# Top-k norm statistics taken in the window phase, reciprocals two sequences at once, and a new step order in the packed attention of two layers

## The chip, the cores and the metric

The kernel runs on one core of one Trainium2 chip. The metric is the device time of one execution in microseconds; each kernel has a median over its runs. The profile and the trace come from one separate profiled execution of the same program.

## The reference

64 sequences of 128 tokens and 128 channels pass through three transformer layers and a final mixture of experts. `T`=128 tokens, `C`=128 channels, `S`=77 context tokens, `H`=16 heads of `D`=8. What bears on the change:

```python
# layer 0
h = _ln(x) * (1 + sc_msa) + sh_msa
x = x + _self_attn(h) * g_msa             # windows of 64 tokens, shifted by 32
h = _ln(x) * (1 + sc_mca) + sh_mca
x = x + _topk_cross_attn(h, ctx) * g_mca  # softmax over the 16 largest of 77 scores
x = x + _swiglu(...) * g_mlp
# layers 1 and 2
x = x + gate_a * (attention(modulate(_ln(x))) @ W_proj + b)      # 128 keys
x = x + attention(_ln(x), keys and values from context) @ W + b  # 77 keys
x = x + gate_m * mlp(modulate(_ln(x)))
```

`_ln` subtracts the mean over the channels and multiplies by one over the root of the variance plus 1e-6.

## The kernel before, in words

The phases follow each other: setup, window attention of layer 0, top-k attention of layer 0, MLP, then twice (layers 1 and 2) a packed attention and an MLP, then the mixture of experts. x stays in SBUF (`r.x`). All phases work on groups of `G`=4 sequences, so there are `NG`=16 groups. Each engine has an instruction list of its own, in one order written out by hand: a body per group with steps `u`, in which pieces of several groups are interleaved; semaphores couple the engines.

**Window and top-k phases** (`attention_phase`). A window body has 8 steps, a top-k body 16. In the top-k phase the vector engine does four MAX8 and four MATCH_REPLACE8 twice in each step (`find_top`), and per body the norm statistics of the group two ahead (`ln_stats`, L743; `ln_variance`, L774 and L777), a reciprocal per sequence (`reciprocals`, L879) and one add to x (L927). GpSimd turns the variance into one over the root (`rstd_of`, L488, then L491 and L493) and multiplies the rows by the reciprocals (`divide_rows`, L515). ScalarE applies the norm (`ln_apply`, L581).

**Packed attention** (`packed_attention_layer`). `NT`=32 groups pass through it: 16 of self attention (128 keys), then the same 16 of cross attention (77 keys). A body has `NS`=8 steps, two to a sequence. In a step TensorE does 8 matmuls of the scores (L1616, into `s_ps`) interleaved with 8 of the transposed scores of the step 7 before (L1631), in 32-row tiles; VectorE reduces the two halves of the scores to maxima (L1491, two TENSOR_REDUCE per step); ScalarE takes the exponentials of the transposed scores (L1374, two per step); TensorE multiplies them with the values (L1656, 16 matmuls). `s_ps` has one buffer for each half, so before it writes a step's scores TensorE waits until both maxima of the step before are taken:

```python
def scores_waits(g, u):
    ...
    after(pe, s_max, 2 * (NS * g + u))
```

Around that, each body has these pieces at fixed steps: transpose of the normed rows (`XT`, L1584), keys (`KP`, L1592), queries (`QP`, L1597) and values (`VP`, L1604) of the group two ahead, transpose of the attention output (`ONT`, L1752), its projection (`PROJ`, L1756), and the transpose back with the add to x (L1681 at step 0, L1527 at step 1). Keys and queries are split in a high and a low part: ScalarE writes the high part (L1349, L1355), VectorE the low part (`low_keys` L1466, `low_queries` L1471); TensorE starts the queries only when the low part of the keys is there, since all use one PSUM bank `l_ps`. At even steps two transposes of output rows (L1667) come too, at odd steps a transpose of the maxima (L1642). SyncE's queue copies keys and queries to their 32-row places: 12 DMAs for keys, 14 for queries in each body (L1267, L1253, L1255). `keep_clock` (L1676) issues matmuls whose result nobody reads: 2, 3, 2 and 2 at steps 0 to 3, after the values and the transposes of that step, into `l_ps`; where no projections come any more, 2 in each step.

Of the kernel before, what the change touches and what calls it, by code (L numbers as in the profile page):

```python
# [29 lines left out]
S = 77  # L30
# [212 lines left out]
def attention_phase(nc, r, layer, kind):  # L243
# [42 lines left out]
    with nc.cleanup_on_exit(), ExitStack() as ctx:  # L286
# [20 lines left out]
        ctx_var = sb("ctx_var", [S, G]) if window else None  # L307
        if split:
# [8 lines left out]
        nmr = sb("nmr", [T, G]) if topk else None  # L317
        orow = sb("orow", [T, 2, H, VM]) if topk else None
# [5 lines left out]
        rden = sb("rden", [T, 2, H])  # L324
# [17 lines left out]
        s_nmr, s_rows = sem("nmr"), sem("rows")  # L342
# [129 lines left out]
        def _(pool):  # L472
# [11 lines left out]
            def rstd_of(g):  # L484
                pool.wait_ge(s_var, g + 1)
                if topk:
                    after(pool, s_xn, g)
                nc.gpsimd.tensor_tensor(rstd[:, :], vareps[:, :], r.neg_half[:, :], ALU.pow).then_inc(s_rstd, 1)  # L488
                if topk:
                    pool.wait_ge(s_rstd, g + 1)  # L490
                    nc.gpsimd.tensor_tensor(nmr[:, :], mv[:, :, 0], rstd[:, :], ALU.mult).then_inc(s_nmr, 1)  # L491
                    after_alone(pool, s_nmr, 2 * g + 1)
                    nc.gpsimd.tensor_scalar(nmr[:, :], nmr[:, :], -1.0, None, ALU.mult).then_inc(s_nmr, 1)  # L493
# [16 lines left out]
            def divide_rows(i, b):  # L510
                m = G * i + b
                if b % G == 0:
                    after(pool, s_onps, i)
                pool.wait_ge(s_rden, m + 1)
                nc.gpsimd.tensor_tensor(on[:, b % G, :].rearrange("p (h d) -> p h d", d=D), orow[:, b % 2, :, 0:D],  # L515
                                        rden[:, b % 2, :].rearrange("p (h a) -> p h a", a=1).broadcast_to([T, H, D]),
                                        ALU.mult).then_inc(s_norm, 1)

            def prologue():
                rstd_of(0)  # L520
                rstd_of(1)

            def body(i, par, first, units, pre, ln):
                for u in range(NS if units else PGT + 1):
# [4 lines left out]
                    if b is not None:  # L529
                        divide_rows(i, b)  # L530
                    if ln and u == AGGR:
                        rstd_of(i + 2)
                    if window and units and u == AGGR + 1:
                        context_rstd(i)

            iterations(pool, body, prologue)

        @block.scalar
        def _(act):
# [36 lines left out]
            def ln_apply(g, bs=range(G)):  # L576
                if bs[0] == 0:
                    after(act, s_xT, g)
                    act.wait_ge(s_nmr, 2 * g + 2)
                for b in bs:  # L580
                    last = nc.scalar.activation(xn[:, b:b + 1, :], r.x[:, bass.ds(G * g + b, 1), :], ACT.Identity,  # L581
                                                scale=rstd[:, b:b + 1], bias=nmr[:, b:b + 1])
# [3 lines left out]
            def rows_out(i, b):  # L586
                m = G * i + b
                after(act, s_norm, m - 1)
                act.wait_ge(s_otr, m + 1)
                nc.scalar.copy(orow[:, b % 2], r_ps[:, :].rearrange("p (h c) -> p h c", c=32)[:, :, 0:VM]  # L590
# [131 lines left out]
        def _(dve):  # L722
# [45 lines left out]

            def ln_variance(g):
                after_alone(dve, s_stats, g + 1)  # L770
                if topk:
                    after_alone(dve, s_nmr, 2 * g)
# [102 lines left out]
            def reciprocals(i, b):  # L875
                m = G * i + b
                after(dve, s_norm, m - 1)
                dve.wait_ge(s_rows, m + 1)
                nc.vector.reciprocal(rden[:, b % 2, :], orow[:, b % 2, :, D]).then_inc(s_rden, 1)  # L879

            def prologue():
                ln_stats(0)
                ln_variance(0)
                if not topk:
                    ln_apply(0)
                low_keys(0)
                low_queries(0)
                ln_stats(1)
                ln_variance(1)
                if not topk:  # L890
                    ln_apply(1)
# [1857 lines left out]
```

## Time and profile before

| | us |
|---|---|
| median of 3 runs (lowest, highest) | 3427.48 (3426.73, 3434.89) |
| the profiled execution's own time | 3441.14 |
| its span | 3439.3 |
| window phase, first to last scores | 38.6 to 429.2 |
| top-k phase, first to last scores | 461.8 to 1214.8 |
| packed attention of layer 1, first to last scores | 1443.3 to 2075.9 |
| packed attention of layer 2, last scores | 2901.6 |
| TensorE busy | 3029.5 (88%) |
| VectorE busy | 2612.0 (76%) |
| ScalarE busy | 2246.9 (65%) |
| GpSimd busy | 1041.2 (30%) |
| mean granted TensorE clock | 0.946 |

Busy times count an instruction from its start to its end, and matmuls are pipelined, so a TensorE that is busy may still issue less than it could: what one piece costs it is read from the start of the piece to the start of the next. The granted clock is a share of 2.4 GHz. PEld is TensorE's weight load, which runs beside the matmuls before it.

### The profile page before, as it was taken

The numbers are of one execution on the slowest core, as the hardware profiler recorded it, in microseconds if no ns is written. First come the engines' busy times: TensorE is split into PE (matmuls) and PEld (weight loads), VectorE is DVE, ScalarE is ACT, GpSimd is POOL, SyncE is SP. The second block draws the span as 40 slices with busy tenths as digits, with TensorE's granted clock in tenths as the row PEclk, the third lists the DMA queues.
The fourth block names the chain that finished last, engine by engine and source line by source line (L and its number), as shares of the span: only waits on it lengthen the run. The fifth ranks groups of instructions, "written<-read, shape, count | busy, mean of one in ns | idle before, by whom it ended". The sixth has DMA issues, their size and how long they took to land. (4 is left out here: it accounts for less than half of the span.)

```text
span 3439.3 us, 93774 instructions
## 1 busy us (share of the span) xinstructions
PE 3029.5 (88%) x31851; PEld 2015.6 (59%) x31851; DVE 2612.0 (76%) x12300; ACT 2246.9 (65%) x5561; POOL 1041.2 (30%) x1278
## 2 busy tenths in 40 slices
PE   5999977777777779799999998989999999889998
PEld 3544444444444457566666665556666666558887
DVE  4878769999999978588887764568887775546665
ACT  2666657777777657367776666647776666646665
POOL 0000046666666656511122211121112221112221
PEclk9999969999989989899999999979999999989999
DMA  1111000000000000144444430034444442000000
GB/s 44 45 51 35 18 10 9 9 9 9 8 8 9 4 1 1 46 102 105 106 107 102 104 96 5 1 92 105 104 106 103 103 103 56 1 32 16 21 21 18
DMA packets 145007, 165.37 MB, mean 48 GB/s; under 512 B 41494, under 2 KB 93974, under 8 KB 144278
## 3 DMA queue, kind: packets, MB, share of 16 engines
q1 hardware_dynamic: 132374, 133.32, 15.4%
q0 software_dynamic: 12160, 26.04, 3.2%
q8 instruction: 260, 4.26, 0.6%
q14 instruction: 213, 1.74, 0.2%
HBM read 18.85 MB, written 4.19 MB: 7 GB/s over the span
## 5 line engine op out<-in xcount | busy, mean ns | idle before, releaser
L1374 ACT ACTIVATE attn_pT<-attn_t 128x512 f32<-128x512 f32 (+1 forms) x1024 | 555.4, 596 | 321.7 <-PE attn_t L1631 321.7
L1491 DVE TENSOR_REDUCE attn_mx<-attn_s 128x4 f32<-128x512 f32 (+1 forms) x1024 | 549.2, 578 | 142.0 <-PE attn_s L1616 141.2
L1616 PEld LDWEIGHTS attn_s<-packed_keys,packed_queries 32*128 32x128 f32 x4096 | 277.3, 190 | 163.6 <-DVE attn_mx L1491 95.6
L659 ACT ACTIVATE topk_prob<-topk_s,topk_nmx 128x77 f32<-128x77 f32 x1024 | 248.3, 326 | 181.8 <-DVE topk_work L840 160.5
L1616 PE MATMUL attn_s<-packed_keys,packed_queries 32*128 32x128 f32 (+1 forms) x4096 | 342.2, 288 | 14.8 <-DVE attn_mx L1491 7.2
L1289 POOL DMA_DIRECT2D packed_queries<-attn_om x256 | 142.8, 558 | 649.3 <-ACT attn_om L1367 645.5
L1023 PE MATMUL topk_s<-kbd,topk_qT 128*128 128x308 f32 x512 | 216.3, 507 | 129.8 <-ACT topk_prob L659 129.5
L1656 PE MATMUL attn_o<-attn_pT,attn_vp 128*18 128x128 f32 (+1 forms) x8192 | 327.1, 278 | 0.0
L503 POOL TENSOR_SCALAR topk_mask<-topk_work 128x308 f32<-128x308 f32 x256 | 250.1, 977 | 239.8 <-DVE topk_work L845 238.6
L1631 PE MATMUL attn_t<-packed_queries,packed_keys 32*128 32x128 f32 (+1 forms) x4096 | 300.4, 264 | 0.0
L1631 PEld LDWEIGHTS attn_t<-packed_queries,packed_keys 32*128 32x128 f32 (+1 forms) x4096 | 227.9, 166 | 4.7 <-ACT attn_pT L1374 3.4
L1676 PE MATMUL attn_l<-packed_keys 128*128 128x512 f32 x636 | 225.6, 444 | 0.7 <-DVE attn_vp L1481 0.7
L840 DVE MATCH_REPLACE8 topk_work<-topk_top,topk_s 128x77 f32<-128x77 f32 x1024 | 220.3, 224 | 0.0
L507 POOL TENSOR_TENSOR topk_prob<-topk_prob,topk_mask 128x308 f32<-128x308 f32 x256 | 213.8, 835 | 21.3
L1656 PEld LDWEIGHTS attn_o<-attn_pT,attn_vp 128*18 128x18 f32 (+1 forms) x8192 | 181.5, 97 | 60.8 <-issue 44.4
L845 DVE MATCH_REPLACE8 topk_work<-topk_top,topk_work 128x77 f32<-128x77 f32 x1024 | 215.4, 219 | 0.0
L1023 PEld LDWEIGHTS topk_s<-kbd,topk_qT 128*128 128x128 f32 x512 | 87.1, 211 | 195.7 <-ACT topk_prob L659 141.8
L1033 PEld LDWEIGHTS topk_t<-ident,topk_prob 128*77 128x77 f32 x1024 | 147.0, 163 | 57.6 <-issue 16.7
L829 DVE MAX8 topk_top<-topk_s 128x8 f32<-128x77 f32 x1024 | 167.1, 222 | 15.9 <-PE topk_s L1023 15.5
L1033 PE MATMUL topk_t<-ident,topk_prob 128*77 128x128 f32 x1024 | 171.3, 295 | 0.9 <-POOL topk_prob L507 0.9
L834 DVE MAX8 topk_top<-topk_work 128x8 f32<-128x77 f32 x1024 | 163.4, 218 | 0.0
L1285 POOL TENSOR_TENSOR attn_rstd<-attn_vareps,neg_half 128x4 f32<-128x4 f32 x64 | 65.8, 1028 | 318.0 <-DVE attn_vareps L1449 318.0
(328 smaller groups left out, 7543.0 us busy)
## 6 DMA issues: line engine op xcount, KB each, us to landing
packed_queries<-attn_qT SPq DMA_DIRECT2D x720, 64.0 KB, 2.2
packed_keys<-attn_kT SPq DMA_DIRECT2D x384, 64.0 KB, 2.1
packed_queries<-attn_om POOLq DMA_DIRECT2D x256, 64.0 KB, 2.3
packed_queries<-zero_rows SPq DMA_DIRECT2D x120, 128.0 KB, 2.7
packed_keys<-attn_kT SPq DMA_DIRECT2D x384, 39.0 KB, 2.3
kbd<-window_kT SPq DMA_DIRECT2D x512, 8.0 KB
kbd<-topk_kT SPq DMA_DIRECT2D x512, 4.8 KB
x_res<-in_x SPq DMA_DIRECT2D x16, 192.0 KB, 2.6
```

What stands on the lines that cost most here:

```text
L503: nc.gpsimd.tensor_scalar(mask[:, u % 2, :], work[:, n % NP, :], NEG / 2, None, ALU.is_le).then_inc(s_mask, 1)
L659: last = nc.scalar.activation(prob[:, n % NP, h * keys:(h + 1) * keys], s_ps[:, u % 2, h * keys:(h + 1) * keys], ACT.Exp, scale=SCALE, bia ...
L840: last = nc.vector.match_replace(wk_[now][:, h, :], top[:, u % 2, h, :], sc[:, h, :], NEG)
L845: last = nc.vector.match_replace(wk_[past][:, h, :], top2[:, c % 2, h, :], wk_[past][:, h, :], NEG)
L1023: last = nc.tensor.matmul(s_ps[:, u % 2, 0:cols], qT[:, par, b * T:(b + 1) * T], r.kbd[:, HU * g:HU * g + HU, b * keys:(b + 1) * keys], st ...
L1033: last = nc.tensor.transpose(t_ps[0:rows, c % 2, j * T:(j + 1) * T], prob[:, n % NP, j * rows:(j + 1) * rows], r.ident[:, :])
L1374: nc.scalar.activation(pT[0:keys, c % 2, h, :], t_ps[0:keys, h, :], ACT.Exp, scale=SCALE).then_inc(s_exp, 1)
L1491: nc.vector.tensor_reduce(mx[:, (c // 2) % 2, 2 * k + h, :], sc, AX.X, ALU.max).then_inc(s_max, 1)
L1616: last = nc.tensor.matmul(s_ps[:, h, k * KW:(k + 1) * KW], r.qp[32 * j:32 * j + 32, buf, k, b * T:(b + 1) * T], r.kp[32 * j:32 * j + 32, b ...
L1631: last = nc.tensor.matmul(t_ps[0:keys, h, k * T:(k + 1) * T], r.kp[32 * j:32 * j + 32, buf, k, b * KW:b * KW + keys], r.qp[32 * j:32 * j + ...
L1656: last = nc.tensor.matmul(o_ps[32 * k:32 * k + 18, v * T:(v + 1) * T], vp[0:keys, buf, b, k, v, a, :], pT[0:keys, c % 2, a, k * T:(k + 1) ...
L1676: nc.tensor.matmul(l_ps[:, :], r.kp[:, buf, 0, 0:T], r.kp[:, buf, 0, :], start=True, stop=True)
```

## The change

Layer 0: the statistics of the top-k norm are taken in the window phase, for the group two bodies before, into buffers that hold all 64 sequences (`next_rstd`, `next_nmr`); the last group's come after the last body. The top-k phase reads them, so its `ln_stats`, `ln_variance` and `rstd_of` are gone, and its prologue projects the first keys before the normed rows. The reciprocals of two sequences are one instruction, and their two row multiplications follow each other.

Layers 1 and 2: `XT` goes from step 3 to 2, `KP` from 5 to 4, `QP` stays at 6, `VP` goes from step 7 to step 0 of the next body. The unread matmuls go from steps 0 to 3 to the odd steps (3, 2, 2, 2), and from the end of a step to its beginning, behind the wait for the maxima, into `s_ps`. VectorE's pieces of the norm move to steps 2, 3, 5 and 7.

```diff
@@ attention_phase: gpsimd @@
+            def next_rstd(g):
+                pool.wait_ge(s_nvar, g + 1)
+                nc.gpsimd.tensor_tensor(r.next_rstd[:, G * g:G * g + G], next_var[:, :], r.neg_half[:, :], ALU.pow
+                                        ).then_inc(s_nrstd, 1)
...
             def divide_rows(i, b):
-                m = G * i + b
-                if b % G == 0:
+                pair = (G * i + b) // 2
+                if b % G == 1:
                     after(pool, s_onps, i)
-                pool.wait_ge(s_rden, m + 1)
...
+                pool.wait_ge(s_rden, pair + 1)
+                for k in range(2):
+                    at = (b - 1 + k) % G
+                    nc.gpsimd.tensor_tensor(on[:, at, :].rearrange("p (h d) -> p h d", d=D), orow[:, at, :, 0:D],
...
@@ attention_phase: scalar @@
             def prologue():
                 if topk:
+                    ln_apply(0)
                     raw_out(0)
+                    keys_out(0, 0)
                     raw_out(1)
-                    ln_apply(0)
                 modulate(0)
-                keys_out(0, 0)
+                if not topk:
+                    keys_out(0, 0)
@@ attention_phase: vector @@
+            def next_statistics(g):
+                dve.wait_ge(s_x, g + 1)
+                for b in range(G):
+                    last = nc.vector.bn_stats(next_stats[:, b, :], r.x[:, G * g + b:G * g + b + 1, :])
+                last.then_inc(s_nst, 1)
+
+            def next_variance(g):
+                dve.wait_ge(s_nst, g + 1)
+                for b in range(G):
+                    last = nc.vector.bn_aggr(next_mv[:, g % 2, b, :], next_stats[:, b, :])
+                last.then_inc(s_nmv, 1)
+                dve.wait_ge(s_nmv, g + 1)
+                after(dve, s_nrstd, g)
+                nc.vector.tensor_scalar(next_var[:, :], next_mv[:, g % 2, :, 1], 1e-6, None, ALU.add).then_inc(s_nvar, 1)
+
+            def next_shift(g):
+                dve.wait_ge(s_nrstd, g + 1)
+                nc.vector.scalar_tensor_tensor(r.next_nmr[:, G * g:G * g + G], next_mv[:, g % 2, :, 0], -1.0,
+                                               r.next_rstd[:, G * g:G * g + G], ALU.mult, ALU.mult).then_inc(s_nnmr, 1)
...
-                nc.vector.reciprocal(rden[:, b % 2, :], orow[:, b % 2, :, D]).then_inc(s_rden, 1)
+                nc.vector.reciprocal(rden[:, pair % 2, :].rearrange("p (k h) -> p k h", h=H), orow[:, at:at + 2, :, D]
+                                     ).then_inc(s_rden, 1)
...
-                    if ln and u in STATS:
+                    if ln and u in STATS and not topk:
...
+                    if window and i > 2 and u == 2:
+                        next_shift(i - 3)
+                    if window and i > 1 and u == 5:
+                        next_statistics(i - 2)
+                    if window and i > 1 and u == 6:
+                        next_variance(i - 2)
...
             iterations(dve, body, prologue)
+            if window:
+                next_shift(NG - 2)
+                next_statistics(NG - 1)
+                next_variance(NG - 1)
+                next_shift(NG - 1)
@@ packed_attention_layer @@
-    XT, KP, QP, VP = 3, 5, 6, 7
+    XT, KP, QP, VP = 2, 4, 6, 0
-    UNREAD = (2, 3, 2, 2)
+    UNREAD = (0, 3, 0, 2, 0, 2, 0, 2)
@@ gpsimd @@
-                    if u == VP and NG <= i + 3 < NT:
-                        stage_context(i + 3)
+                    if u == 1 and NG <= i + 2 < NT:
+                        stage_context(i + 2)
@@ vector @@
                         if u == 2:
-                            ln_stats(i + 3, (0, 1, 2))
+                            ln_stats(i + 3)
                         if u == 3:
-                            ln_stats(i + 3, (3,))
                             ln_variance(i + 3)
-                        if u == XT + 1:
+                        if u == 5:
                             ln_apply(i + 3, (0, 1))
-                    if u == 0 and i > 0 and there(before, left, 2):
-                        ln_apply(i + 2, (2, 3))
+                        if u == 7:
+                            ln_apply(i + 3, (2, 3))
...
-                        if u == VP:
-                            values_out(i + 2, (m3 + 2) % 3)
+                    if u == VP and i > 0 and there(before, left, 1):
+                        values_out(i + 1, (m3 + 1) % 3)
@@ tensor @@
-            def keep_clock(g, buf, count):
-                pe.wait_ge(s_v, min(g + 2, NT))
+            def keep_clock(buf, count):
                 for _ in range(count):
-                    nc.tensor.matmul(l_ps[:, :], r.kp[:, buf, 0, 0:T], r.kp[:, buf, 0, :], start=True, stop=True)
+                    nc.tensor.matmul(s_ps[:, 0, :], r.kp[:, buf, 0, 0:T], r.kp[:, buf, 0, :], start=True, stop=True)
...
                     if now:
                         scores_waits(i, u)
+                        keep_clock(m3, UNREAD[u] if there(before, left, 2) else 2)
+                    elif back:
+                        after(pe, s_max, 2 * NS * NT)
+                        keep_clock((m3 + dg) % 3, 2)
...
-                    if now and u < len(UNREAD):
-                        keep_clock(i, m3, UNREAD[u])
-                    elif not there(before, left, 2) and (now or back):
-                        keep_clock(i, m3, 2)
...
-                        if u == VP:
-                            project_values(i + 2)
+                    if u == VP and i > 0 and there(before, left, 1):
+                        project_values(i + 1)
```

## Rows read from the trace of the kernel before

**Rows 1.** Busy time by stretch (start:end, length, PE, PEld, DVE, ACT, POOL, clock, DMA, GB/s).

```profile
38.00:437.00 399.00, 378.32 (x3960) 187.31 (x3956) 301.85 (x867) 239.88 (x485) 30.14 (x30) 0.97 0.14 35
500.00:1180.00 680.00, 513.14 (x3918) 313.84 (x3919) 679.32 (x5708) 511.32 (x1796) 456.56 (x557) 0.92 0.03 8
...
1500.00:1740.00 240.00, 224.28 (x3582) 150.74 (x3578) 209.41 (x633) 175.03 (x366) 37.79 (x59) 1.00 0.43 107
1820.00:2050.00 230.00, 218.44 (x3609) 151.67 (x3601) 165.86 (x618) 151.76 (x296) 45.02 (x69) 0.99 0.42 103
```

**Rows 2.** Timeline of VectorE in one top-k body (start us, us, instruction).

```profile
706.96 0.28 DVE L743 BATCH_NORM_STATS2 topk_stats<-x_res 128x6 f32<-128x128 f32 x1
707.16 0.66 DVE L829 MAX8 topk_top<-topk_s 128x8 f32<-128x77 f32 x4
...
713.18 0.23 DVE L879 RECIPROCAL topk_rden<-topk_orow 128x16 f32<-128x16 f32 x1
713.34 0.60 DVE L829 MAX8 topk_top<-topk_s 128x8 f32<-128x77 f32 x4
...
721.92 0.37 DVE L774 BATCH_NORM_AGGREGATE topk_mv<-topk_stats 128x2 f32<-128x6 f32 x4
...
722.47 0.67 DVE L829 MAX8 topk_top<-topk_s 128x8 f32<-128x77 f32 x4
```

**Rows 3.** Timeline from the window phase's last add to the first MAX8.

```profile
443.39 0.69 DVE L927 TENSOR_TENSOR x_res<-window_r,x_res 128x512 f32<-128x512 f32 x1 [6.50 <-PE window_r L1132]
...
447.86 1.01 POOL L488 TENSOR_TENSOR topk_rstd<-topk_vareps,neg_half 128x4 f32<-128x4 f32 x1 [0.86 <-DVE topk_vareps L777]
...
463.33 0.68 DVE L829 MAX8 topk_top<-topk_s 128x8 f32<-128x77 f32 x4 [13.17 <-PE topk_s L1023]
```

**Rows 4.** Key projections, 1475 to 2080 (layer 1): count, ns, first and last start.

```profile
L1592 PE MATMUL attn_l<-attn_ctxs,weights x32: 426/427/428, 1744.2 to 2036.1; 128*128 128x312 f32 x32
...
L1592 PE MATMUL attn_l<-attn_hT,weights x26: 592/594/595, 1480.6 to 1724.6; 128*128 128x512 f32 x26
```

**Rows 5.** The same, 2295 to 2870 (layer 2).

```profile
L1592 PE MATMUL attn_l<-attn_ctxs,weights x32: 426/427/428, 2565.9 to 2861.6; 128*128 128x312 f32 x32
...
L1592 PE MATMUL attn_l<-attn_hT,weights x26: 592/594/595, 2299.8 to 2545.0; 128*128 128x512 f32 x26
```

**Rows 6.** Waits, 1500 to 1740, self attention (total us, times, longest).

```profile
PEld attn_s L1616 <- DVE attn_mx L1491: 25.1, 69, 0.8
...
PE attn_l L1597 <- DVE attn_kT L1466: 12.9, 12, 1.3
```

**Rows 7.** Waits, 1820 to 2050, cross attention.

```profile
PE attn_l L1597 <- DVE attn_kT L1466: 7.1, 12, 0.6
...
PE attn_l L1604 <- DVE attn_qT L1471: 4.0, 5, 1.4
```

**Rows 8.** Timeline of TensorE over step 1 of a self attention body.

```profile
1612.18 0.32 PE L1616 MATMUL attn_s<-packed_keys,packed_queries 32*128 32x128 f32 x1
...
1613.38 0.94 PE L1676 MATMUL attn_l<-packed_keys 128*128 128x512 f32 x3
1614.29 0.33 PE L1616 MATMUL attn_s<-packed_keys,packed_queries 32*128 32x128 f32 x1
```

**Rows 9.** Timeline of VectorE over the same step.

```profile
1612.94 1.29 DVE L1491 TENSOR_REDUCE attn_mx<-attn_s 128x4 f32<-128x512 f32 x2 [0.40 <-PE attn_s L1616]
```

**Rows 10.** Step 1 of a cross attention body: TensorE.

```profile
1927.37 0.30 PE L1616 MATMUL attn_s<-packed_keys,packed_queries 32*128 32x78 f32 x1
...
1928.54 0.94 PE L1676 MATMUL attn_l<-packed_keys 128*128 128x512 f32 x3
```

**Rows 11.** The same step: VectorE.

```profile
1928.11 0.86 DVE L1491 TENSOR_REDUCE attn_mx<-attn_s 128x4 f32<-128x308 f32 x2 [0.80 <-PE attn_s L1616]
```

**Rows 12.** SyncE's DMA queue over one body (start, us, transfer, count).

```profile
1564.39 8.82 SPq L1267 DMA_DIRECT2D packed_keys<-attn_kT  x12
...
1582.03 0.64 SPq L1255 DMA_DIRECT2D packed_queries<-zero_rows  x1
```

More of the change, by code:

```diff
@@ L307, in attention_phase @@
         ctx_var = sb("ctx_var", [S, G]) if window else None
+        next_stats = sb("next_stats", [T, G, 6]) if window else None
+        next_mv = sb("next_mv", [T, 2, G, 2]) if window else None
+        next_var = sb("next_var", [T, G]) if window else None
         if split:
@@ L340, in attention_phase @@
         s_mask = sem("mask")
-        s_nmr, s_rows = sem("nmr"), sem("rows")
+        s_rows = sem("rows")
+        s_nst, s_nmv, s_nvar, s_nrstd, s_nnmr = sem("nst"), sem("nmv"), sem("nvar"), sem("nrstd"), sem("nnmr")
         s_oT, s_otr, s_rden, s_norm = sem("oT"), sem("otr"), sem("rden"), sem("norm")
@@ L528, in body @@
                     b = sequence_hooks(u, first, units, 1) if topk else None
-                    if b is not None:
+                    if b is not None and b % 2 == 1:
                         divide_rows(i, b)
-                    if ln and u == AGGR:
+                    if ln and u == AGGR and not topk:
                         rstd_of(i + 2)
+                    if window and i > 1 and u == 7:
+                        next_rstd(i - 2)
                     if window and units and u == AGGR + 1:
@@ L587, in rows_out @@
                 m = G * i + b
-                after(act, s_norm, m - 1)
+                after(act, s_norm, m - G + 1)
                 act.wait_ge(s_otr, m + 1)
-                nc.scalar.copy(orow[:, b % 2], r_ps[:, :].rearrange("p (h c) -> p h c", c=32)[:, :, 0:VM]
+                nc.scalar.copy(orow[:, b % G], r_ps[:, :].rearrange("p (h c) -> p h c", c=32)[:, :, 0:VM]
                                ).then_inc(s_rows, 1)
@@ L906, in body @@
                         values_out(i + 1, 1 - par, u - VP)
[L907 removed]
+                    if ln and u in STATS and not topk:
                         ln_stats(i + 2, [b for b in range(G) if STATS[b] == u])
[L909 removed]
+                    if ln and u == AGGR and not topk:
                         ln_variance(i + 2)
+                    if window and i > 2 and u == 2:
[4 more added lines that the diff above has]
+                        next_variance(i - 2)
                     if window and units and u in (0, 1):
@@ L919, in body @@
                     b = sequence_hooks(u, first, units, 1 if topk else 0)
-                    if b is not None and topk:
+                    if b is not None and topk and b % 2 == 1:
                         reciprocals(i, b)
-                    elif b is not None:
+                    elif b is not None and not topk:
                         normalise(i, b)
@@ L930, in _ @@
             iterations(dve, body, prologue)
+            if window:
+                next_shift(NG - 2)
+                next_statistics(NG - 1)
+                next_variance(NG - 1)
+                next_shift(NG - 1)
         @block.tensor
@@ L960, in transpose_xn @@
                 after(pe, s_pg, g - 2)
+                if topk and g == 0:
+                    pe.wait_ge(s_kT, 1)
                 pe.wait_ge(s_xn, g + 1)
@@ L968, in project_keys @@
                     pe.wait_ge(s_raw, g + 1)
-                pe.wait_ge(s_hT, g + 1)
+                if not topk or g > 0:
+                    pe.wait_ge(s_hT, g + 1)
                 nc.tensor.matmul(l_ps[:, 0:G * KW], wk, source[:, G * g:G * g + G, :] if cross else hT[:, :],
@@ L974, in project_queries @@
                 pe.wait_ge(s_klo if split else s_kT, g + 1)
+                if topk and g == 0:
+                    pe.wait_ge(s_hT, 1)
                 nc.tensor.matmul(l_ps[:, :], wq, hT[:, :], start=True, stop=True).then_inc(s_qps, 1)
@@ L1081, in prologue @@
                     transpose_context(0)
+                    project_keys(0)
                     transpose_context(1)
                 transpose_xn(0)
-                project_keys(0)
+                if not topk:
+                    project_keys(0)
                 project_queries(0)
```

44 lines of the change are left out of this document (19 added, 25 removed).

## The prediction

> **What bounds the kernel now.** I read the busy time by stretch first, because the change touches three phases with different limits. In it the reader is to compare the engines within a row [rows 1]. The window phase has TensorE busy for 378 of 399 us and VectorE for 302: TensorE bounds it. The top-k phase has VectorE busy for 679.3 of 680 us, TensorE for 513, ScalarE for 511 and GpSimd for 457: VectorE alone bounds it, and each slot taken from it is time. In the packed attention TensorE is busy for 224 of 240 us (self) and 218 of 230 (cross), VectorE for 209 and 166, at a granted clock of 1.00 and 0.99, that is nearly all at 2.4 GHz.
>
> Then the timeline of VectorE in the top-k phase, for the slots of the instructions that go: start to next start, since the busy time of one overlaps the next [rows 2]. Then the starts of the key projections, one pair of matmuls per body, which give the length of a body: self (1724.6 - 1480.6 - 0.4) / 12 = 20.3 us in layer 1 and (2545.0 - 2299.8 - 0.4) / 12 = 20.4 in layer 2; cross (2036.1 - 1744.2 - 0.3) / 15 = 19.4 and (2861.6 - 2565.9 - 0.3) / 15 = 19.7 [rows 4, 5]. (The 0.4 and 0.3 are there because the last start is that of the pair's second matmul.) Then the waits [rows 6, 7] and one step of TensorE beside the same step of VectorE [rows 8 to 11], which decide the prediction. Last SyncE's queue [rows 12].
>
> **Top-k phase: shorter by about 22 us.** A bn_stats takes a slot of 707.16 - 706.96 = 0.20 us, the four aggregates with the addition of eps 722.47 - 721.92 = 0.55 [rows 2]. A body loses 4 x 0.20 + 0.55 = 1.35 us, and 14 bodies have this work (groups 2 to 15): 18.9 us. A reciprocal takes 713.34 - 713.18 = 0.16 us; the MAX8s behind it take 0.60 in place of 0.66, so I count 0.11. 64 of them become 32 of twice the elements: 32 x 0.11 = 3.5 us, less some tenths for the elements. Together 22 us; from below 18.9 (a pair costs as much as two), from above 18.9 + 32 x 0.16 = 24, and one us more if VectorE's waits on GpSimd for the norm go too. Can the others follow a step that is 3% shorter? The nearest has 75% [rows 1], so yes. The second row multiplication now comes later in GpSimd's list; it is a sequence late for the transposes of the output, which can hold TensorE for a few tenths, and TensorE has a quarter of the phase free.
>
> **Window phase: 0 to 5 us longer, I take 1.** It gets the same 1.35 us and a shift (about 0.15, the smallest operations' slot) per body, for 15 bodies 22 us of VectorE, of which it has 97 free [rows 1]. TensorE waits on VectorE only for scores two steps back, so a piece of 0.8 us is caught up in the next steps. If a fifth of it showed it would be 5 us.
>
> **Between the phases: 0.** The last group's statistics now stand behind the last add to x: stats 0.8, aggregates 0.55, pow 1.0, shift 0.2 with the hops between engines: about 2.9 us before the window phase can end [rows 2, 3]. The top-k prologue has 463.33 - 444.08 = 19.3 us from the add to the first MAX8 [rows 3]. It no longer has this chain, and the key projection and its copy run before the normed rows are there. The context's DMA and transposes, which stood beside the norm, are now first; I take the gain as 3 us too, with 2 us either way.
>
> **Packed attention: longer by about 80 us.** What is meant to go is TensorE's wait for the keys' low part, one step after the keys: 12.9 us for 12 bodies in self, and 7.1 + 4.0 in cross, where the values wait for the queries too [rows 6, 7]. At two steps' distance these waits are gone: -1.1 and -0.9 us per body. All of it lies on the path, since TensorE sets the pace. TensorE's own work in a body, with the same 9 unread matmuls, is then about 20.3 - 1.1 - 0.2 = 19.0 in self (0.2 to 0.4 for short waits on the maxima that the end of the matmuls before hides) and 19.5 - 0.9 - 0.3 = 18.3 in cross.
>
> What takes its place comes from where the pieces land. After the change *all* pieces (transposes, keys, queries, values, output) are at even steps. An odd step has scores, values, one small transpose, and the unread matmuls, which now stand *behind* the wait for the last maxima and *before* the scores. The next step can't begin before this step's maxima are taken. That ring is seen in step 1: scores start at 1612.18, the two reductions at 1612.94 and take 1.29 us, and the next scores start at 1614.29: 2.11 us [rows 8, 9]. In the meantime TensorE had 1613.38 - 1612.18 = 1.20 us of work and three unread matmuls of together 0.91, which filled the ring to the brim at no cost. Ahead of the scores they are outside the ring: an odd step lasts 2.11 us plus its unread matmuls (0.91, and 0.6 for two), and TensorE stands idle for 2.11 - 1.20 = 0.9 us in it. An even step has 2.4 us or more of work, so that the maxima are ready at its end and hide nothing. Four odd steps: 4 x 0.9 = 3.6, I take 3.3 because the small transpose partly overlaps. A self body: 19.0 + 3.3 = 22.3 us, +2.0 in layer 1 and +1.9 in layer 2.
>
> In cross the ring is shorter: scores at 1927.37, reductions at 1928.11 for 0.86, and about 0.06 to the next scores: 1.66 us, against 1928.54 - 1927.37 = 1.17 of work [rows 10, 11]. Idle 0.45 x 4 = 1.8: 18.3 + 1.8 = 20.1 us, +0.7 in layer 1 and +0.4 in layer 2.
>
> The sum: 16 x 2.0 + 16 x 1.9 (self) = 62; 14 x 0.7 + 14 x 0.4 (cross) = 15; the last two bodies of each layer, with two unread matmuls in every step ahead of the scores, 4 x about 1.2 = 5. Together 82. Bounds: if half of the idle time is hidden (VectorE late at the even steps), 62 bodies or so gain 1.0 and pay 1.3: about +25. If all four odd steps have the full 0.9 and 0.49, +110. What is late next is VectorE's own sum, about 18 us a self body, which has room, and SyncE's queue: 26 DMA issues take 1582.67 - 1564.39 = 18.3 us [rows 12]. It is nearly as long as a body and would be the floor if bodies became shorter; at 20 to 22 us it is not. The norm's pieces on VectorE are evenly spread (each odd step some 1.2 us beside the maxima), so I count them at nothing; if they delayed the maxima of the even steps by 0.4 us, TensorE's even steps, of 2.4 us and more, still cover it.
>
> **Sum.** -22 + 1 + 0 + 82 = +61 us on the profiled execution's 3441.1. That execution is 14 us above the median shown, so the difference is applied to the median: 3427.5 + 61 = 3488; for the unsettled starts of the layers, where the spread-out unread matmuls may keep the clock up, I take 4 off: 3484.
>
> **Rivals.** *A, faster: the idle time is there already.* If TensorE, when it comes to an odd step, already waits for the maxima because VectorE is behind, the moved matmuls cost nothing and the step distance pays in full. The row for it: the weight load of the scores waits for the maxima 69 times for 25.1 us in 12 bodies [rows 6]. Against it: these are the short ends of a ring already filled, and an even step after the change is longer than the ring. It decides if VectorE is 0.6 us late at odd steps. Then self goes to about 19.2 and cross to 18.7 (SyncE's floor near): -1.1 x 32 - 0.8 x 28 = -58, with top-k -80: 3350; with half of it 3375. *B, half the idle time:* +25 - 22: 3431, no change. *C, the clock falls.* TensorE is then busy for some 84% of a self body; the top-k phase, with 513 of 680 us (75%), has 0.92 where the attention has 1.00 [rows 1], so some of its time is at 1.2 GHz. At a mean of 0.96 TensorE's work grows by 4%: 0.04 x 19 x 60 = +45 on top: 3530.
>
> The Trainium skill (TensorE: Matmul & The Clock Gate, section "A second HAM failure mode: psum-queue depth-cycling") says that short idle times between groups of matmuls can make the clock swing between its two levels. By that rule C would be the case; the row of the top-k phase bears it out at a busy share of 75%, the attention rows at 93% don't.
>
> **How the numbers follow.** My forecast (attention +60 to +105) has 0.70, C 0.10, A 0.12, B 0.08. Faster 0.13, within 0.3% (3417 to 3438) 0.06, slower 0.81; 0.3% is about what a measurement of this kernel can tell from no change. The range: attention from +25 up to C gives 3430 to 3530.
>
> **What would show it.** In the timeline of an odd step: two or three unread matmuls directly before the scores, and after the small transpose 0.8 to 0.9 us without a matmul, ended by the reduction. Waits of the scores on the maxima of some 3 us a body in self, while those of the queries on the keys' low part are gone. Key projections 22.3 and 20.1 us apart. The top-k phase 22 us shorter with VectorE still at 99%. The prediction is wrong if the odd steps show no idle time (then VectorE was the bound), or if the clock in the attention is below 0.98.

## The result, and the profile after

The changed kernel takes 3591.2 us (median of 4 runs, 3579.5 to 3595.2) against 3429.9 us of the kernel before on the same chip: a ratio of 1.045, 95% interval 1.042 to 1.048. The direction was forecast, the size was not: 3484 was predicted, with 3530 as the upper end.

The profiled execution of the changed kernel has a span of 3590.0 us against 3439.3 before, 150.7 more, at the same mean granted clock of 0.946. From the timelines of both, read at the starts of the scores:

| | before, us | after, us | difference |
|---|---|---|---|
| top-k phase, first to last scores | 461.8 to 1214.8 (753.0) | 460.6 to 1194.2 (733.6) | -19.4 |
| first scores of layer 1's attention | 1443.3 | 1423.1 | -20.2 |
| layer 1, first to last scores | 632.3 | 725.1 | +92.8 |
| from there to layer 2's first scores | 184.3 | 187.0 | +2.7 |
| layer 2, first to last scores | 641.4 | 714.6 | +73.2 |
| behind it | 538.0 | 540.2 | +2.2 |

So layer 0's part gave what the prediction says (20.2 against 21), and the packed attention cost 166 us in place of 82. First the windows of the changed kernel, for the stretches of [rows 1]: start and end, length, then busy us and count for each engine, the granted clock, the DMA share and GB/s.

```profile
38.00:437.00 399.00, 377.93 (x3960) 186.97 (x3956) 317.69 (x1016) 237.48 (x486) 44.77 (x45) 0.98 0.14 35
...
500.00:1180.00 680.00, 515.12 (x4013) 314.30 (x4012) 680.00 (x5712) 521.09 (x1835) 450.51 (x533) 0.94 0.03 8
...
1500.00:1740.00 240.00, 209.84 (x3183) 136.54 (x3178) 186.79 (x571) 154.97 (x327) 34.35 (x53) 0.99 0.39 93
1820.00:2050.00 230.00, 206.38 (x3118) 138.20 (x3119) 147.46 (x561) 133.92 (x263) 41.44 (x62) 0.96 0.38 91
```

The window phase has 15.8 us more of VectorE than [rows 1] and is no longer for it; in the top-k phase VectorE still has no gap. In the attention every engine is less busy than before: TensorE 210 of 240 us in place of 224, VectorE 187 in place of 209. Less work in the same time and no engine fuller is the picture of a wait in a ring. And the cross stretch has a granted clock of 0.96, where it had 0.99 [rows 1].

Next the median length of each step of a body, from the start of its scores to the start of the next step's, over the bodies with all pieces (made from the timelines of both kernels, layer 1). The last column is the sum of the eight. After the change, the unread matmuls of an odd step stand ahead of its scores, and so in the interval of the even step before it.

```
step                  0     1     2     3     4     5     6     7   body
self,  before      2.47  2.11  2.52  2.28  2.58  2.24  3.55  2.33  20.07
self,  after       3.83  2.11  3.18  2.11  3.95  2.11  3.10  2.30  22.68
cross, before      2.43  2.05  2.45  2.25  2.41  1.99  3.07  2.34  18.99
cross, after       3.70  1.99  3.04  1.99  3.60  1.99  3.07  1.99  21.37
```

The step of [rows 8] and [rows 10] is step 1. After the change every odd step has one and the same length, whatever piece of work the step before had: 2.11 us in self (2.30 at step 7, which had 2.33 before too), 1.99 in cross. That is a floor. Here is what makes it, TensorE in an odd step of a self body (start, length, line, operation, and in brackets the idle time before it):

```profile
1671.85 0.73 PE L1730 MATMUL attn_s<-packed_keys 128*128 128x512 f32 x2
1672.52 0.32 PE L1671 MATMUL attn_s<-packed_keys,packed_queries 32*128 32x128 f32 x1
...
1673.11 0.63 PE L1711 MATMUL attn_o<-attn_pT,attn_vp 128*18 128x128 f32 x16
1673.67 0.28 PE L1697 MATMUL attn_o<-ident,attn_mq 128*32 128x128 f32 x1
1674.82 0.29 PE L1671 MATMUL attn_s<-packed_keys,packed_queries 32*128 32x128 f32 x1 [0.86 <-DMA packed_keys<-attn_kT]
```

and VectorE in the same step:

```profile
1673.28 1.29 DVE L1547 TENSOR_REDUCE attn_mx<-attn_s 128x4 f32<-128x512 f32 x2 [0.54 <-PE attn_s L1671]
```

The two unread matmuls stand directly before the scores, at 1671.85; after the small transpose at 1673.67 TensorE has nothing for 0.86 us. The reductions end at 1673.28 + 1.29 = 1674.57, and 0.25 later the scores start: the ring of [rows 8, 9] with nothing in it, 1674.82 - 1672.52 = 2.30. (This is step 7. The releaser in the bracket names a DMA of the keys; by the order of the code the keys that the next body needs were moved a body earlier. What the other 0.19 us of this step are, no run shows. The other three steps have 2.11 and name the maxima.) Step 1 of an earlier body is such a step, 1635.39 - 1633.29 = 2.10, with the scores 0.05 after the maxima:

```profile
1633.29 0.32 PE L1671 MATMUL attn_s<-packed_keys,packed_queries 32*128 32x128 f32 x1
...
1635.39 0.32 PE L1671 MATMUL attn_s<-packed_keys,packed_queries 32*128 32x128 f32 x1 [0.66 <-DVE attn_mx L1547]
```

```profile
1634.05 1.29 DVE L1547 TENSOR_REDUCE attn_mx<-attn_s 128x4 f32<-128x512 f32 x2 [1.50 <-PE attn_s L1671]
```

The waits of the self stretch (1500 to 1760; us in all, times, longest) answer [rows 6]:

```profile
PEld attn_s L1671 <- DVE attn_mx L1547: 29.3, 34, 1.2
PE attn_s L1671 <- DVE attn_mx L1547: 22.9, 34, 1.0
...
PE attn_s L1671 <- DMA packed_keys<-attn_kT: 9.5, 11, 0.9
```

34 + 11 = 45 waits for 22.9 + 9.5 = 32.4 us, for 260 / 22.7 = 11.5 bodies: four a body, 2.8 us. The wait of the queries for the keys' low part, for which the change was made, is in no row any more. In the cross stretch (1900 to 2080) the chief wait of TensorE is another one than [rows 7] had, and than the prediction named:

```profile
PE attn_s L1671 <- ACT attn_pT L1430: 15.9, 28, 0.6
```

The releaser is ScalarE's exponential. One odd step of a cross body, TensorE, then VectorE and ScalarE:

```profile
1921.41 0.30 PE L1671 MATMUL attn_s<-packed_keys,packed_queries 32*128 32x78 f32 x1
1921.42 0.28 PE L1686 MATMUL attn_t<-packed_queries,packed_keys 32*77 32x128 f32 x1
...
1922.55 0.28 PE L1697 MATMUL attn_o<-ident,attn_mq 128*32 128x128 f32 x1
1923.40 0.27 PE L1671 MATMUL attn_s<-packed_keys,packed_queries 32*128 32x78 f32 x1 [0.57 <-DMA packed_keys<-attn_kT]
```

```profile
1922.16 0.86 DVE L1547 TENSOR_REDUCE attn_mx<-attn_s 128x4 f32<-128x308 f32 x2 [0.52 <-PE attn_s L1671]
```

```profile
1922.18 1.08 ACT L1430 ACTIVATE attn_pT<-attn_t 77x512 f32<-77x512 f32 x2 [1.33 <-PE attn_t L1686]
```

The reductions are done at 1923.02, the exponentials at 1923.26. The scores start only at 1923.40, 0.38 after the maxima and 0.14 after the exponentials. The transposed scores (attn_t) go into `t_ps`, which the exponentials empty; in cross they work on 512 columns where the reductions have 308, so theirs is the longer ring: 1.99 us and not 1.66.

### The profile page after: what moved, and what is told of

It reads as the page before. It is cut to its first block and busy times, and to the rows that moved or that the text cites. A ratio compares the mean times of both kernels' runs of the same rounds, so it can differ in the third digit from the quotient of the medians.

```text
span 3590.0 us, 93637 instructions
## 1 busy us (share of the span) xinstructions
PE 3094.3 (86%) x31847; PEld 2031.2 (57%) x31847; DVE 2609.2 (73%) x12284; ACT 2242.0 (62%) x5561; POOL 1036.2 (29%) x1246
## 5 line engine op out<-in xcount | busy, mean ns | idle before, releaser
L1730 PE MATMUL attn_s<-packed_keys 128*128 128x512 f32 x632 | 228.8, 451 | 9.0 <-DVE attn_mx L1547 8.5
```

The source lines that it names most:

```text
L1730: nc.tensor.matmul(s_ps[:, 0, :], r.kp[:, buf, 0, 0:T], r.kp[:, buf, 0, :], start=True, stop=True)
```

## The experiments

Ratios are against the kernel before on the same chip, with 95% intervals. Steps are medians in bodies that run at 2.4 GHz throughout, a body's length is the sum of its steps' medians, and "mean" is the mean over the 14 self or cross bodies of a layer behind the first two.

### The parts: layer 0 alone, the attention alone

Layer 0's part of the diff on the kernel before.

> The change to layer 0 alone, with the packed attention of before. My theory: the top-k phase is bounded by VectorE, so the slots taken from it are time, and the window phase hides what it gets: 20 us faster than before (3410, ratio 0.994); the top-k phase 733 us from first to last scores in place of 753. Rival: the gain seen in the changed kernel's trace is partly paid in the window phase or between the phases: less than 10 us faster.

Measured: 3408.1 us, ratio 0.996 (0.995 to 0.997). First to last top-k scores 732.9 us, the bodies of the packed attention as before (20.07 and 18.92). The attention's part on the old layer 0:

> The attention part of the change alone, on layer 0 as it was. If the parts add up, it is the changed kernel plus the 15 to 20 us that layer 0's part gave alone: about 175 us over the kernel before, a ratio of 1.051, with self bodies of 22.7 us and cross bodies of 21.4 us where undisturbed, and 753 us from the first to the last scores of the top-k phase. Rival: layer 0's part has a share in the loss, by the phase in which the packed layers start; then the ratio is that of the changed kernel, 1.045, or below it.

Measured: 3611.8 us, ratio 1.052 (1.049 to 1.055), bodies of 22.69 and 21.37 us. The product 0.996 x 1.052 = 1.048 is at the edge of the changed kernel's interval: the parts add up, and the loss is the attention's.

### Only the place of the unread matmuls

The changed kernel with them at the end of the same odd steps, in the same number, behind waits that are met by then:

```diff
-                    nc.tensor.matmul(s_ps[:, 0, :], r.kp[:, buf, 0, 0:T], r.kp[:, buf, 0, :], start=True, stop=True)
+                    nc.tensor.matmul(to[:, :], r.kp[:, buf, 0, 0:T], r.kp[:, buf, 0, :], start=True, stop=True)
...
-                        keep_clock(m3, UNREAD[u] if there(before, left, 2) else 2)
...
+                    if now and (u % 2 or not there(before, left, 2)) or back and not now:
+                        keep_clock(i, u, m3 if now else (m3 - 1) % 3, there(before, left, 2))
```

(`to` is `l_ps`, at step 3 `f_ps`.)

> The changed kernel with the unread matmuls at the end of their odd steps again, in a bank that is free then, in place of behind the wait for the maxima. My theory: behind the wait they are outside the ring of scores and maxima, at the end they fill TensorE's idle time in it. A self body goes from 22.7 us to 19.8 to 20.1, a cross body from 21.4 (22.4 with low clock stretches) to 18.9, odd steps stay 2.1 and 2.0 us; in all 3591 - 2.7 x 32 - 3.0 x 28 = about 3400 to 3430. Rival, the step order itself (all pieces at even steps) is what costs: the bodies lose no more than 1 us and the kernel stays above 3530.

Measured: 3414.9 us, ratio 0.998 (0.996 to 1.000). The odd steps are again 2.11 and 1.99 us (2.33 at step 7 of self; in cross 2.05 at step 1 and 2.2 to 2.4 at step 7), but the even ones lose what they had gained: steps 0, 2, 4 and 6 of self have 2.90, 2.52, 3.29 and 2.43 in place of 3.83, 3.18, 3.95 and 3.10. A self body is 19.80 and a cross body about 19.0. The whole loss is gone, from a ratio of 1.045 to 0.998: the place of the nine matmuls is its cause. Against layer 0's part alone on the same chip (3408.1 us) the new order of the steps itself shows no gain.

### None, and fewer

No unread matmul in the bodies at all:

```diff
-                        keep_clock(m3, UNREAD[u] if there(before, left, 2) else 2)
+                        keep_clock(m3, 0)
```

> The changed kernel with no unread matmuls in the attention bodies. If their time behind the wait is all they cost: as with them at the end of the steps, 3400 to 3430, with the granted clock still 1.00 in the attention. Rival, they are needed for the clock: the granted clock in the attention falls under 0.9, and the matmuls at 1.2 GHz give back more than 60 us: above 3480.

Measured: 3464.3 us, ratio 1.013 (1.011 to 1.015), at a mean granted clock of 0.922. Its windows, one in self and one in cross:

```profile
1500.00:1720.00 220.00, 186.81 (x3190) 128.13 (x3185) 193.24 (x592) 160.37 (x338) 35.41 (x55) 0.98 0.44 107
1850.00:2050.00 200.00, 177.73 (x2906) 125.11 (x2904) 135.80 (x510) 127.02 (x247) 36.53 (x57) 0.89 0.40 97
```

At 2.4 GHz a self body has the same 19.81 us as with nine at the end of the steps: there they are free. But the cross stretch has a clock of 0.89, its bodies a mean of 20.0 (layer 1) and 21.6 us (layer 2) where 18.69 stand at full clock, which few of them have. The matmuls that nobody reads pay for themselves by the clock: without them all four runs have a mean of 0.922 to 0.928, with nine at the end of the steps the ten runs have 0.941 to 0.954. The profiled executions of the two differ by 49 us, of which 40 lie in layer 2's attention (667.2 against 626.9 us from first to last scores); there the cross bodies have a mean of 21.6 against 19.5. In layer 1 the kernel with nine has a clock of 0.92 and a mean of 20.7 in cross, no better than without. Then five in place of nine, behind the wait for the maxima as in the change: `UNREAD = (0, 2, 0, 1, 0, 1, 0, 1)`.

> The changed kernel with 5 unread matmuls a body behind the wait in place of 9 (2, 1, 1, 1 at the odd steps). If each costs its own length behind the wait, a body loses 4 x 0.3 = 1.2 us: self 22.7 to 21.4, cross 21.4 to 20.2, 60 x 1.2 = 72 us less, 3520. Rival: with fewer of them the clock falls more often and takes it back: above 3560.

Measured: 3525.2 us, ratio 1.028 (1.027 to 1.030). The odd steps stay at 2.11 and 1.99 and each even step loses 0.23: self 21.75 (-0.93), cross 20.44 (-0.93). An unread matmul outside the ring costs 0.23 us when one is taken from a row of two or three, less than the 0.3 that a third of [rows 8]'s 0.94 makes. A whole row of three costs 0.93 and one of two 0.66, as the even steps of the changed kernel against those with the matmuls at the end show. 60 bodies of 0.93 are 56 us, and the ratio's step from 1.045 to 1.028 is 57.

### The old order, with the unread matmuls behind the wait

The kernel before, its pieces where they were, and only `keep_clock` moved to the beginning of steps 0 to 3, behind `scores_waits`, into `s_ps`.

> The kernel before, step order as it was, with only the place of the unread matmuls changed: at steps 0 to 3 behind the wait for the maxima. My theory: each of these steps then lasts a ring (2.11 us self, 1.99 cross) plus its unread matmuls: self bodies 20.2 to 22.2, cross 19.5 to 21.1, in all about 120 us slower than before, 3549. Rival (step order costs, the place doesn't): within 20 us of before.

Measured: 3523.6 us, ratio 1.030 (1.028 to 1.032); self bodies 22.04 us (+1.97), cross bodies 19.89 (+0.9, where +2.1 was expected), and 58.5 and 57.5 us in place of 46.6 and 49.2 from a layer's first scores to step 1 of its third body. So in self the edit costs its price without any move of pieces; in cross less than was expected. The reason stands in the trace. Step 1 of a cross body of this run, whose first scores start at 2752.80:

```profile
2753.57 1.07 ACT L1374 ACTIVATE attn_pT<-attn_t 77x512 f32<-77x512 f32 x2 [1.75 <-PE attn_t L1631]
2754.46 0.73 PE L1673 MATMUL attn_s<-packed_keys 128*128 128x512 f32 x2 [0.24 <-DVE attn_mx L1491]
2755.13 0.30 PE L1616 MATMUL attn_s<-packed_keys,packed_queries 32*128 32x78 f32 x1
```

The unread matmuls wait for the maxima alone, so they start at 2754.46, while ScalarE is at the exponentials until 2754.64. The step lasts 2.32 us, which is 1.66 for the ring of the maxima and 0.66 for two unread matmuls, and not the 1.99 + 0.66 that the expectation took; in self the same step has 2.77 = 2.11 + 0.66.

### The second ring

The changed kernel, with the cross exponentials over 256 of their 512 columns. Half of the exponentials of cross attention is left out.

```diff
+                    w = 2 * T if at(g)[0].cross else BANK
-                    nc.scalar.activation(pT[0:keys, c % 2, h, :], t_ps[0:keys, h, :], ACT.Exp, scale=SCALE
+                    nc.scalar.activation(pT[0:keys, c % 2, h, 0:w], t_ps[0:keys, h, 0:w], ACT.Exp, scale=SCALE
```

> The changed kernel, with the exponentials of the cross attention taken over 256 of 512 columns (half of that work is left out). My theory: in cross the odd steps of 1.99 us are closed by a second ring that my prediction missed, transposed scores to exponentials and back; with half the columns the first ring (scores and maxima, 1.66 us) is the longer one. Cross odd steps go from 1.99 to 1.66 to 1.70 us, a cross body from 21.4 to about 20.1, self unchanged; at least 1.3 x 28 = 36 us less than the changed kernel, 3550. Rival, the odd steps are closed by something else (the maxima): they stay at 1.99 us, and the time at 3590.

Measured: 3535.0 us, ratio 1.031 (1.029 to 1.033). ScalarE in two steps of a cross body:

```profile
1918.69 0.65 ACT L1431 ACTIVATE attn_pT<-attn_t 77x256 f32<-77x256 f32 x2 [1.33 <-PE attn_t L1687]
1919.59 0.48 ACT L1423 COPY attn_om<-attn_o 128x384 f32<-128x384 f32 x1 [0.25 <-PE attn_o L1698]
1920.52 0.65 ACT L1431 ACTIVATE attn_pT<-attn_t 77x256 f32<-77x256 f32 x2 [0.45 <-PE attn_t L1687]
```

The pair takes 0.65 in place of 1.08 us, and the odd step goes from 1.99 to 1.66 (1.86 at step 7): 0.33 for 0.43 less of ScalarE. It stops at 1.66, to the hundredth what the prediction had worked out for the ring of the maxima. The self bodies stay at 22.68. So both rings are there, and the longer one counts. A cross body has 20.39 us, 0.98 less (step 2 is longer by 0.14), and the clock changes with it:

```profile
1820.00:2050.00 230.00, 217.02 (x3429) 145.53 (x3428) 160.34 (x610) 111.48 (x284) 45.19 (x68) 1.00 0.41 99
```

No cross body of either layer has a piece at 1.2 GHz in this execution, and the mean clocks of all four runs, 0.954 to 0.960, lie above the changed kernel's 0.946 to 0.952. The means of the cross bodies are 20.48 and 20.51 us in place of 22.74 and 22.12, 54 us for 28 bodies: 27 by the shorter body and the rest by the clock.

### Pieces at the odd steps

If an odd step has 0.8 to 0.9 us of idle time, work belongs there. The changed kernel with `XT, KP, QP, VP = 3, 5, 7, 1` (the output's pieces stay at 2 and 4), VectorE's follow-up pieces a step later, and five unread matmuls a body, ahead of the output rows' transposes or at the end of step 3, where the engine waits for no maxima:

```diff
-    XT, KP, QP, VP = 2, 4, 6, 0
-    UNREAD = (0, 3, 0, 2, 0, 2, 0, 2)
+    XT, KP, QP, VP = 3, 5, 7, 1
+    UNREAD = (1, 0, 1, 1, 0, 0, 2, 0)
```

> Changed layer 0, and a new step order made from the cause: transpose, keys, queries and values at the odd steps (3, 5, 7, 1 of the next body), two steps apart, where TensorE idles in the ring; low parts and values of VectorE one step later; 5 unread matmuls at steps 0, 2, 3 and 6, before the transposes of the output rows or before the transpose at step 3. TensorE's work at odd steps then fills the ring (1.20 + 0.5 to 1.0 us of 2.11). A body is 18.5 to 19.2 us (SyncE's queue of 18.3 us is the floor), 45 us less than with the attention of before: 3360. Rival, the clock falls with 5 unread matmuls, or VectorE's 17.9 us of work collide with the ring: 3400 or more.

Measured: 3399.2 us, ratio 0.992 (0.990 to 0.995); cross bodies 18.24, self bodies 19.78 in place of 18.5 to 19.2. One step in self has 3.38 us. Its TensorE and its ScalarE:

```profile
1641.79 0.50 PE L1729 MATMUL attn_r<-packed_keys 128*128 128x512 f32 x1
1643.04 0.66 PE L1734 MATMUL attn_f<-ident,attn_pg 128*128 128x128 f32 x4 [0.75 <-ACT attn_pg L1448]
```

```profile
1641.25 0.69 ACT L1411 ACTIVATE attn_qT<-attn_l,bias_cols 128x512 fp32r<-128x512 f32 x1 [0.58 <-PE attn_l L1653]
1641.84 1.15 ACT L1448 ACTIVATE attn_pg<-attn_f,gate_bias,mod 128x128 f32<-128x128 f32 x3
```

The four transposes back from the projection wait 0.75 us for three pieces of `attn_pg`, which stand behind the copy of the queries at step 7; that copy is now there too. With eight unread matmuls, `UNREAD = (2, 0, 2, 2, 0, 0, 2, 0)`:

> The same with 8 unread matmuls (2 at each of the steps 0, 2, 3 and 6). TensorE's work is 0.9 us longer: body 19.0 to 19.6 us, 3375 to 3390 if the clock is 1.00 in both. Rival, the clock matters more than the work: this one is the faster of the two.

Measured: 3403.1 us, ratio 0.992 (0.990 to 0.994), bodies 20.07 and 18.63. Then ScalarE's pieces of `attn_pg` a step earlier in both:

```diff
-                        if u == PROJ + 3:
+                        if u == PROJ + 2:
```

> The kernel of e7 with one edit: ScalarE's second and third pieces of the gated projection stand one step earlier in its list. In e7 a self body has one step of 3.38 us in which the transposes back from the projection stand idle for 0.83 us until that piece is there. If the piece's place in the list is the cause, that step falls to about 2.6 us, self bodies go from 19.78 to about 19.0 us, cross bodies (whose projection is one piece, elsewhere in the list) stay at 18.2: 32 x 0.8 = -25 us against e7, a ratio of about 0.985 to the kernel before. Rival: VectorE or the exponentials' ring takes the place of the wait, and the body stays above 19.5; then within 8 us of e7.

> e9's edit in the kernel of e8, with eight unread matmuls in a body in place of four. Undisturbed bodies: self 20.07 - 0.8 = 19.3, cross 18.6. If two extra unread matmuls cost 0.2 to 0.3 us in the bodies and save stretches at 1.2 GHz in cross, it lands within 6 us of e9; if the shorter self bodies bring stretches at 1.2 GHz, which show as single bodies of 22 us or more, e9 suffers more of them and e10 is ahead.

(The number that this last text calls four is five: 1 + 1 + 1 + 2.) Measured, with five and with eight: 3400.0 us (10 runs, 3378 to 3432), ratio 0.991 (0.987 to 0.994), and 3404.4 us (4 runs, 3373 to 3426), ratio 0.990 (0.984 to 0.995). The step falls from 3.38 to 2.26 and the self body to 18.75 as expected (19.15 with eight). Yet the 25 us don't show in the time: it now varies by 53 us from run to run, where the kernel before varies by 22. The time goes with the clock: of the ten runs with five, the three fastest (3378 to 3380 us) have a mean granted clock of 0.946 to 0.953, the three slowest (3419 to 3432 us) 0.931 to 0.935. The profile says where it is lost. Windows of the kernel with eight, whose profiled execution is the slowest of its four (layer 2's cross attention, before, in and after the stretch), then of that with five:

```profile
2690.00:2720.00 30.00, 29.21 (x478) 19.75 (x474) 23.18 (x91) 21.09 (x41) 7.39 (x11) 1.00 0.45 105
2730.00:2820.00 90.00, 89.60 (x943) 59.64 (x945) 44.43 (x168) 40.44 (x78) 13.28 (x20) 0.59 0.28 68
2825.00:2870.00 45.00, 42.34 (x728) 29.34 (x722) 29.29 (x105) 29.71 (x58) 6.72 (x11) 1.00 0.42 102
```

```profile
2745.00:2770.00 25.00, 22.82 (x373) 14.82 (x372) 19.02 (x73) 17.05 (x35) 4.66 (x8) 1.00 0.46 110
2774.00:2826.00 52.00, 47.89 (x611) 32.86 (x608) 23.74 (x84) 24.95 (x49) 5.12 (x9) 0.72 0.28 69
```

For some 74 us TensorE has 1.2 GHz in the first, though it is busy for 89.6 of 90 us there; two bodies take 32.3 us each. The mean granted clock is 0.938 and 0.935 where e7's and e8's have 0.949. Why the stretches fall where they do is open: no run tells it. What is shown is that the kernels with odd pieces are faster than the one before, by 0.8 to 1.0%. Against layer 0's part alone (0.995 to 0.997) only two intervals lie apart, and barely: that of the first kernel with eight, 0.990 to 0.994, and that of the second with five, 0.987 to 0.994.

## Why the prediction was wrong in size and right in direction

**Top-k, window and between: right.** -20.2 us against -22 + 1 + 0 = -21, and -15 in the runs of that part alone. The top-k phase gave 19.4, the lower one of the two bounds (18.9): a pair of reciprocals takes a slot of 0.26 us in the trace after, where two took 2 x 0.16.

**The wait for the keys' low part: right.** It is gone, and yet it was worth less than the 1.1 us a self body that the prediction took: with the unread matmuls at the end of the steps the self body is 19.80, only 0.3 shorter than before (20.07), since the odd steps end at their ring's 2.11 us.

**Self bodies: the mechanism right, the size a little low.** Predicted 22.3 us, measured 22.68; the idle time at the odd steps is there, 2.8 us a body in the waits, and 0.2 more stand at step 7. The 28 bodies behind the first two cost 38.5 + 34.1 = 72.6 us where +2.0 or +1.9 each make 55; 28 x 0.38 = 11 of the difference are in every body, the rest in single longer ones: five of the 28 have a piece at 1.2 GHz, where none had one before. The last two bodies of each layer cost 7 for 5, the first two 4 for 8.

**Cross bodies: the step that failed.** "In cross the ring is shorter: ... 1.66 us ... Idle 0.45 x 4 = 1.8": the odd step was sized by the ring from the scores over VectorE's reductions alone, since [rows 10, 11] show only these. It is closed by the transposed scores and ScalarE's exponentials, 1.99 us, and stands idle for 1.99 - 1.17 = 0.8. The term was 15 us; the 28 bodies behind the first two measured 47.2 + 35.3 = 82.5. At 2.4 GHz a body is 21.37 us for 20.1, that is 28 x 1.27 = 36 us more. The four floors differ by 4 x 0.33 = 1.3 us; the run with half the exponentials, where only the ring that the prediction knew is left, gained 0.98 a body, so 27 of the 36 are the second ring. Its body of 20.39 us is the one to set beside the predicted 20.1: the other 8 us are TensorE's own work and short waits, which the 18.3 had too low, and no run separates them. The trace of before had this ring at the very step that was read, on ScalarE, whose timeline was not read:

```profile
1928.13 1.08 ACT L1374 ACTIVATE attn_pT<-attn_t 77x512 f32<-77x512 f32 x2 [1.35 <-PE attn_t L1631]
...
1930.18 1.08 ACT L1374 ACTIVATE attn_pT<-attn_t 77x512 f32<-77x512 f32 x2 [0.60 <-PE attn_t L1631]
```

From pair to pair there are 2.05 us in step 1, and step 5 in the table above has 1.99.

**The clock: rival C, in cross only.** The mean bodies are 22.74 (layer 1) and 22.12 us (layer 2) for 21.37 at 2.4 GHz: 14 x 1.37 + 14 x 0.75 = 30 us. (Before, the means were 0.4 and 0.6 above the body at full clock too, but only 3.4 and 6.8 us of these stretches were at 1.2 GHz, against 41.1 and 20.5 after. Those were in the main longer bodies at 2.4 GHz, and the prediction's 19.4 and 19.7 contain them.) A clock below 0.98 in the attention was also one of the prediction's own signs of being wrong. The stretches at 1.2 GHz are gone in the run with half the exponentials, so this loss too hangs on the second ring, at least in that execution. Four bodies of layer 2's cross attention in a row, one window for each:

```profile
2793.00:2816.00 23.00, 20.72 (x305) 13.64 (x304) 14.32 (x54) 12.93 (x25) 4.01 (x7) 0.93 0.36 87
2816.00:2837.30 21.30, 19.03 (x304) 12.99 (x303) 14.27 (x54) 12.81 (x25) 4.02 (x6) 1.00 0.39 95
2837.30:2860.30 23.00, 20.72 (x304) 13.63 (x303) 14.27 (x54) 12.93 (x25) 3.98 (x6) 0.93 0.36 86
2860.30:2881.70 21.40, 19.13 (x308) 13.02 (x307) 14.28 (x54) 12.81 (x25) 3.99 (x6) 1.00 0.39 95
```

Every second body has a piece at 1.2 GHz and lasts 23.0 us in place of 21.3. In self, with TensorE busy for 87% and idle for 0.9 us at the odd steps, the clock is 0.99; in cross, with 90% and 0.8 us, 0.96. The rule of the Trainium skill that the prediction set beside this rival (TensorE: Matmul & The Clock Gate, section "A second HAM failure mode: psum-queue depth-cycling") fits the cross rows and not the self rows, and nothing measured here tells why. Idle time alone does not sort the stretches: with nine unread matmuls at the end of the steps, layer 1's cross stretch has 0.92 with TensorE busy for 96%.

Together: cross 82.5 - 15 = 67 (27 the second ring, 8 the rest of the body, 30 the clock), self 18, the last two bodies 2, the first two -4: 83, against a miss of 166 - 82 = 84. The range failed with it: its upper end was rival C alone, and no bound let a longer ring stand in cross. Rivals A and B are out: the idle time was not there before, and all four odd steps have it now.

## What to carry to other kernels

- When work is moved from behind a wait to ahead of what the wait guards, it leaves the ring, and its whole length is added wherever the ring was the bound; what matters is on which side of the wait filler work stands, not how much there is. Here the nine matmuls took the ratio to 1.045 on one side of it and left it at 0.998 on the other, 161 us. Filler that waits for one ring alone can still run beside the other, longer one, as in the cross bodies of the old order.
- Size a ring by *every* consumer of what a step writes. A step with two outputs (here `s_ps` to VectorE and `t_ps` to ScalarE) has two rings, and the longer one counts; look for a step in the trace that has little else in it, and its length is the floor.
- Put pieces of work in the steps that have idle time in their ring. Where bodies get shorter this way, look at the granted clock over several runs before counting the gain.

## What was not expected of the hardware

- In layer 2's cross attention of the changed kernel the pieces at 1.2 GHz recur every 44.4 us, two bodies of the loop. In the kernels with odd pieces single long stretches appear, the longest of some 74 us, with TensorE busy for 89.6 of 90 us. They are no property of the new order alone: with the attention of before and only layer 0 changed, one cross body of layer 1 lasts 31.2 us, in a stretch of 30.7 us at 1.2 GHz.
- Nine unread matmuls a body cost nothing in self at the end of the steps (19.80 us with, 19.81 without), but without them the kernel takes 49 us more, at a mean granted clock of 0.922 to 0.928 over its runs against 0.941 to 0.954. The cross stretch of layer 1 has 0.89 without them, 0.92 with them at the end of the steps and 0.96 ahead of the scores.
